# Two sequences' adapters joined, with one gate made in the call ahead, and the shared tiles' down products of the experts issued in sequence

## What is computed

```python
g = einsum('td,edf->tef', xt, Wg); u = einsum('td,edf->tef', xt, Wu)
h = silu(g) * u
y = einsum('tef,efd->ted', h, Wd)
out = einsum('ted,te->td', y, combine)
```

```python
gate = softmax(x.mean(axis=1) @ gate_w.T)
top_w, top_i = top_k(gate, 2); top_w = top_w / (top_w.sum(-1) + 1e-8)
h = gelu(x @ Wd[top_i] + bd[top_i], approximate=False) * top_w
out = h @ Wu[top_i] + (top_w * bu[top_i]).sum()
```

## Time and profile before

| | before |
|---|---|
| median of 3 runs | 3846.09 us (3843.22 to 3848.20) |
| the profiled execution | 3842.31 us |
| its span, first to last instruction | 3840.4 us |
| TensorE busy | 3608.5 us, 94% |
| VectorE busy | 2288.8 us, 60% |
| ScalarE busy | 1735.2 us, 45% |
| GpSimd busy | 824.6 us, 21% |
| mean granted clock of TensorE | 0.994 |

### The profile page before, as it was taken

The page is one execution under the profiler, slowest core; times in us unless marked ns, Lnnn a source line. Parts: engine busy times, 40 slices in busy tenths (PEclk is TensorE's granted clock), DMA queues, the critical chain, the costliest instruction groups (busy, mean ns, idle before and its releaser), DMA issues.

```text
span 3840.4 us, 78752 instructions
## 1 busy us (share of the span) xinstructions
PE 3608.5 (94%) x31071; PEld 2406.5 (63%) x31167; DVE 2288.8 (60%) x7514; ACT 1735.2 (45%) x3546; POOL 824.6 (21%) x1374
## 2 busy tenths in 40 slices
PE   6999999988999999998899999999889999999988
PEld 3656567666565667766556566776655656677665
DVE  4546455677654645577755554557675555455876
ACT  2425333466442523356644252335664335233656
POOL 3203023311210302332021030333302102033330
PEclk8999999999999999999999999999999999999999
DMA  3000000000000000000000000000000000000000
GB/s 88 1 1 2 1 1 1 2 1 2 13 1 1 2 1 1 1 2 2 1 13 1 1 2 1 1 1 2 2 7 8 1 1 1 1 1 1 2 2 9
DMA packets 27032, 17.47 MB, mean 5 GB/s; under 512 B 9425, under 2 KB 26274, under 8 KB 26658
## 3 DMA queue, kind: packets, MB, share of 16 engines
q1 hardware_dynamic: 26658, 12.32, 1.2%
HBM read 10.22 MB, written 2.10 MB: 3 GB/s over the span
## 4 chain that ended last, share of the span: by engine, by line
PE 71%; DVE 11%; POOL 7%; ACT 6%; issue 3%; SPq 1%; DVEq 0%; another core or an unknown queue 0%
PE banks L1237 9%; PE banks L1199 8%; PE banks L1204 8%; PE banks L1049 5%; PE banks L1088 5%; POOL work L564 5%; PE banks L1103 4%; PE banks L1028 3%; PE banks L1291 3%; PE banks L1499 3%; PE banks L1353 2%; ACT work L872 2%; ACT work L866 2%; PE banks L1512 2%; DVE work L1973 2%
## 5 line engine op out<-in xcount | busy, mean ns | idle before, releaser
L1684 DVE CUSTOM_DVE_ANT_0 work<-banks,mask_row 128x512 f32<-128x512 f32 (+3 forms) x1024 | 433.9, 486 | 279.3 <-PE banks L1049 279.2
L719 ACT ACTIVATE work<-banks 128x512 f32<-128x512 f32 x352 | 210.2, 597 | 672.2 <-PE banks L1199 657.0
L1775 DVE TENSOR_TENSOR work<-work,banks 128x512 f32<-128x512 f32 x352 | 242.1, 688 | 444.8 <-PE banks L1204 423.5
L520 POOL TENSOR_TENSOR rstd<-rstd,half 128x4 f32<-128x4 f32 x65 | 65.6, 1009 | 1948.2 <-DVE rstd L1608 1948.2
L742 ACT ACTIVATE work<-banks 128x384 f32<-128x384 f32 (+1 forms) x768 | 358.8, 534 | 252.2 <-PE banks L1088 251.6
L1237 PEld LDWEIGHTS banks<-wd,work 128*128 128x128 f32 (+2 forms) x4096 | 357.5, 189 | 179.9 <-issue 179.9
L1088 PE MATMUL banks<-work 32*128 32x512 f32 (+3 forms) x2048 | 443.7, 464 | 6.5 <-DVE work L1684 3.9
L1049 PE MATMUL banks<-work 32*128 32x384 f32 (+3 forms) x2048 | 405.2, 456 | 11.9 <-ACT work L728 6.4
L1237 PE MATMUL banks<-wd,work 128*128 128x128 f32 (+2 forms) x4096 | 376.6, 279 | 0.0
L531 POOL TENSOR_SCALAR_AFFINE_SELECT work<-work 128x128 f32<-128x128 f32 (+1 forms) x768 | 253.4, 333 | 458.8 <-ACT work L742 435.5
L1088 PEld LDWEIGHTS banks<-work 32*128 32x128 f32 x2048 | 243.0, 183 | 76.8 <-ACT work L742 39.4
(11 more groups left out here) (320 smaller groups left out, 6627.2 us busy)
## 6 DMA issues: line engine op xcount, KB each, us to landing
x_a<-in_L_attn_a_x_dram SPq DMA_DIRECT2D x5, 256.0 KB, 2.9
x_b<-in_L_attn_a_x_dram SPq DMA_DIRECT2D x4, 256.0 KB, 3.9
wg<-in_L_ffn_Wg_dram SPq DMA_DIRECT2D x2, 512.0 KB
wu<-in_L_ffn_Wu_dram SPq DMA_DIRECT2D x2, 512.0 KB
wd<-in_L_ffn_Wd_dram SPq DMA_DIRECT2D x16, 64.0 KB
out_dram<-x_a SPq DMA_DIRECT2D x4, 256.0 KB
out_dram<-x_b SPq DMA_DIRECT2D x4, 256.0 KB
wk_l<-in_L_attn_a_Wk_dram SPq DMA_DIRECT2D x1, 512.0 KB, 3.6
```

The source lines that it names most:

```text
L1684: m = eng.tensor_tensor_reduce(out=summed[:, k % 2, col:col + N], in0=bank(bk)[:, col:col + N], in1=mask_row[:, T - N:T], scale=1.0, scala ...
```

## The change

- **Adapters joined.** `pe_adapters`, `act_adapters` and `adapters` issue both calls of a pair as one piece. TensorE: down products of a, transpose of a's mix, six fills, the norm's transposes of b, bias and up products of three token tiles of a, gate product of b, the last up tile of a, down products of b, transpose of b's mix, bias and up products of b, and then the norm's transposes of the call behind. At the turn's end six fills stand before those.
- **a's gate in the call ahead.** `gate_pool`, `gate_logits`, `gate_rank` and `gate_weights` of call 0 are issued inside the second linear attention (`lin`, n = 1), those of call 2 at the end of the second relative attention (`rel`, n = 1), with the gate product (`gate_products`) on TensorE and Exp (`gate_exp`) on ScalarE in the same calls. The gate's buffers get places outside those calls' own. VectorE's rank and weights of call 2 stand ahead of the relative attention's addition to `x_b`.
- **Bias by TensorE.** The mixed bias starts the accumulation of each of the four token tiles (two instructions each); VectorE adds one bank of 512 columns to x, instead of the bias and two halves.
- **Shared tiles in sequence.** `DOWN_BEHIND` puts the down products of tiles 0, 1 and 2 behind the up product of tile 4, and those of 11, 12 and 13 behind that of tile 15. All others keep their lag of two tiles.

```diff
@@ -99,6 +99,10 @@
 NTILE = len(TILES)
 LAST = {e: max(i for i, parts in enumerate(TILES) if any(q[0] == e for q in parts)) for e in range(E)}
 DOWN_LAG = 2
+DOWN_BEHIND = [[] for _ in range(NTILE + 1)]
+for i in range(NTILE):
+    DOWN_BEHIND[min(4 + NTILE // 2 * (i // (NTILE // 2)) if len(TILES[i]) > 1 else i + DOWN_LAG, NTILE)].append(i)
 HSLOTS = 12

 LAYERS = ["attn_a", "moe_1", "attn_b", "moe_2", "lin_attn", "adapter_1", "rel_attn", "adapter_2"]
...
@@ -793,6 +792,8 @@
                     eng.activation(l_sq[:, i // 2 % 2, :], dst, ACT.Square).then_inc(l_sqr, 1)
                 if i == NC2 + 3:
                     act_norm(eng, lin_call(n) + 1, 7)
+            if n == 1:
+                gate_exp(eng, 0)
             eng.wait_ge(l_ssk, NC2 * n + NT)
             eng.activation(l_inv[:, 1, :, 0:H // 2], l_ssum[:, 1, :, 0:H // 2], ACT.Sqrt).then_inc(l_norm, 1)
             for i in range(NT):
...
-            eng.activation(d_wT[0:E, :], bank(6)[0:E, 0:P], ACT.Copy).then_inc(d_wTs, 1)
-            act_norm(eng, adapter_call(n) + 1, 0)
+            eng.activation(g["ex"], g["lg"], ACT.Exp, bias=g["negm"][:, 0:1],
+                           accum_out=g["z"][:, 0:1]).then_inc(d_exs, 1)
+        def act_adapters(eng, n):
+            def hidden_rows(m):
+                for k in range(KD):
+                    eng.wait_ge(d_dn, KD * m + k + 1)
+                    eng.activation(d_hids[:, m % 2, k, :], bank(k), ACT.Gelu, bias=down_b[:, k:k + 1]).then_inc(d_hs, 1)
+            def mix_column(m):
+                eng.wait_ge(d_wTp, m + 1)
+                eng.activation(gates[m // 2]["wT"][0:E, m % 2, :], bank(6)[0:E, 0:P], ACT.Copy).then_inc(d_wTs, 1)
+            hidden_rows(n)
+            mix_column(n)
+            act_norm(eng, adapter_call(n + 1), 7)
+            gate_exp(eng, n + 1)
+            hidden_rows(n + 1)
+            mix_column(n + 1)
+            act_norm(eng, adapter_call(n + 1) + 1, 0)

         def act_rel(eng, n):
             act_parts(eng, n, float(HD) ** -0.5)
...
@@ -885,6 +900,8 @@
                 if i >= 4 and i % 2 == 0:
                     group_columns(eng, n, NG * (4 + n) + i // 2 - 2, 7, a_pv, NG * n + i // 2 - 1)
             group_columns(eng, n, NG * (5 + n) - 1, 7, a_pv, NG * (n + 1))
+            if n == 1:
+                gate_exp(eng, 2)
             eng.wait_ge(a_oT, 4 + n + 1)
             eng.activation(xnTs[n % 2][:, :], bank(0), ACT.Copy).then_inc(a_oTs, 1)

...
@@ -1244,15 +1259,15 @@
                 if i >= 2 or n % 2 == 1:
                     moe_gate(eng, n, i)
                     moe_up(eng, n, i)
-                if i >= DOWN_LAG:
-                    down(i - DOWN_LAG)
+                for k in DOWN_BEHIND[i]:
+                    down(k)
                 if i == 9:
                     eng.wait_ge(m_acc, E * n + 1)
                     pe_norm(eng, moe_call(n) + 1, 7)
                 if i == 11 and n % 2 == 0:
                     moe_logits(eng, n + 1, 7)
-            for i in range(NTILE - DOWN_LAG, NTILE):
-                down(i)
+            for k in DOWN_BEHIND[NTILE]:
+                down(k)

         def pe_lin(eng, n):
             xnT = xnTs[n % 2]
...
@@ -1303,12 +1318,17 @@
                     eng.wait_ge(l_ssc, n + 1)
                 elif i == NT + 1:
                     eng.wait_ge(xnT_ok, lin_call(n) + 1)
+                    if n == 1:
+                        eng.wait_ge(d_lgs, 1)
                 elif i >= 2:
                     eng.wait_ge(l_vr, NC2 * n + i - 1)
                 eng.matmul(bank(value_bank(i)), xnT[:, P * (i % NT):P * (i % NT) + P],
                            wv_l[:, 512 * (i // NT):512 * (i // NT) + 512],
                            start=True, stop=True).then_inc(l_vp, 1)

+            if n == 1:
+                eng.wait_ge(xnT_ok, lin_call(n) + 1)
+                gate_products(eng, 0, 7)
             for i in range(NT):
                 key_rows(NT + i)
                 if i == 0:
...
+            def down(m):
+                eng.wait_ge(xnT_ok, adapter_call(m))
+                for k in range(KD):
+                    if m == 2 and k == 1:
+                        eng.wait_ge(d_lgs, m + 1)
+                    eng.matmul(bank(k), downT[:, k, :], xnTs[m % 2][:, :], start=True, stop=True).then_inc(d_dn, 1)
+            def mix_column(m):
+                eng.wait_ge(d_ws, m + 1)
+                eng.transpose(bank(6)[0:E, 0:P], gates[m // 2]["w"][:, m % 2, :], ident[:, :]).then_inc(d_wTp, 1)
+            def up(m, tiles):
+                out = [bank(4 + m % 2)[:, P * t:P * t + P] for t in range(NT)]
+                if tiles[0] == 0:
+                    eng.wait_ge(d_wTs, m + 1)
+                    for t in range(NT):
+                        eng.matmul(out[t], gates[m // 2]["wT"][0:E, m % 2, :], up_b[:, :], start=(t == 0), stop=False,
+                                   skip_group_check=True)
+                for t in tiles:
+                    for k in range(KD):
+                        i = eng.matmul(out[t], d_hids[:, m % 2, k, P * t:P * t + P],
+                                       gates[m // 2]["up"][:, m % 2, k, :], start=False, stop=(k == KD - 1),
+                                       skip_group_check=True)
+                if t == NT - 1:
+                    i.then_inc(d_y, 1)
+            down(n)
+            mix_column(n)
+            fill(eng, 5 if n == 0 else 7, 6)
+            pe_norm(eng, adapter_call(n + 1), 7)
             eng.wait_ge(d_hs, KD * (n + 1))
-            if adapter_call(n) + 1 < CALLS:
-                pe_norm(eng, adapter_call(n) + 1, 0)
             eng.wait_ge(d_ups, n + 1)
-            for t in range(NT):
-                o = bank(4 + t // 2)[:, P * (t % 2):P * (t % 2) + P]
-                for k in range(KD):
-                    m = eng.matmul(o, d_hid[:, k, P * t:P * t + P], d_up[:, k, :], start=(k == 0), stop=(k == KD - 1))
-                if t % 2 == 1:
-                    m.then_inc(d_y, 1)
-                if t == 0:
-                    eng.wait_ge(d_wTs, n + 1)
-                    eng.matmul(bank(7)[:, 0:P], d_wT[0:E, :], up_b[:, :], start=True, stop=True).then_inc(d_bias, 1)
-            if adapter_call(n) + 1 == CALLS:
+            up(n, (0, 1, 2))
+            eng.wait_ge(xnT_ok, adapter_call(n + 1))
+            gate_products(eng, n + 1, 7)
+            up(n, (3,))
+            down(n + 1)
+            mix_column(n + 1)
+            eng.wait_ge(d_hs, KD * (n + 2))
+            eng.wait_ge(d_ups, n + 2)
+            up(n + 1, (0, 1, 2, 3))
+            if adapter_call(n + 1) + 1 == CALLS:
                 fill(eng, 6, 6)
-                pe_norm(eng, CALLS, 0)
+            pe_norm(eng, adapter_call(n + 1) + 1, 0)

         def pe_rel(eng, n, w):
             pe_project(eng, n, w)
...
@@ -1541,6 +1580,8 @@
                 if i >= 2:
                     columns(2 * i - 3)
             weigh(NG - 1)
+            if n == 1:
+                gate_products(eng, 2, 1)
             group_rows(eng, n, NG * (5 + n) - 1, 7)
             pe_out(eng, 4 + n, rel_call(n), w[:, 3, :], bp_row, 0, lambda: fill(eng, 3, 2))

...
@@ -1822,6 +1861,10 @@
                     eng.tensor_copy(l_k[:, t, 512 * half:512 * half + 512], bank(2 + i % 2)).then_inc(l_kr, 1)
                     if i >= 1:
                         reduce_keys(i - 1)
+                    if n == 1 and i == 2:
+                        gate_pool(0)
+                    if n == 1 and i == 3:
+                        gate_logits(0, 7)
                     if i == NT + 1:
                         eng.wait_ge(l_ss, NC2 * n + NC2)
                         eng.tensor_copy(l_ssum[:, 0, :, :].rearrange("p t h -> p (t h)"),
...
                         scale_out(c - 1)
+                    if n == 1 and c == 4:
+                        gate_rank(0)
+                    if n == 1 and c == 5:
+                        gate_weights(0)
...
+            def gate_pool(n):
+                g = gates[n // 2]
                 eng.wait_ge(xnT_ok, adapter_call(n))
-                link(eng.tensor_reduce(pooled[:, 0:1], xnT[:, :], AX.X, ALU.add))
-                eng.tensor_scalar(pool_rep[:, :], pooled[:, 0:1].to_broadcast([P, P]), 1.0 / T, None,
+                link(eng.tensor_reduce(g["pooled"], xnTs[n % 2][:, :], AX.X, ALU.add))
+                eng.tensor_scalar(g["rep"], g["pooled"].to_broadcast([P, P]), 1.0 / T, None,
                                   ALU.mult).then_inc(d_pool, 1)
-                if adapter_call(n) + 1 < CALLS:
-                    norm_stats(adapter_call(n) + 1)
+            def gate_logits(n, bk):
+                g = gates[n // 2]
                 eng.wait_ge(d_gate_ok, n + 1)
...
+                link(eng.tensor_copy(g["lg"], bank(bk)[:, 0:E]))
+                eng.tensor_reduce(g["negm"], g["lg"], AX.X, ALU.max, negate=True).then_inc(d_lgs, 1)
+            def gate_rank(n):
+                g = gates[n // 2]
...
+            def gate_weights(n):
+                g = gates[n // 2]
```

(23 more changed lines are left out.)

120 lines of the change are left out of this document (38 added, 82 removed).

## The result

The changed kernel takes 3794.2 us (median of 4 runs, 3788.8 to 3799.2) against 3846.5 (4 runs): ratio 0.9865, 95% interval 0.9851 to 0.9878. Forecast were 3791 us, a range of 3776 to 3817, and "faster". Timed once more with the experiments it took 3796.9 against 3844.4, ratio 0.9874 (0.9859 to 0.9889). The profiled execution of the table's "after" took 3799.2 us.

The account below looks back on a forecast made before the run. The prediction took TensorE, busy 94% of the span, and the gaps between its instructions as the bound. Pairs 22.4, turn's ends 16.8 and experts 16 made 55 us, giving a median of 3791 us, range 3776 to 3817.

Parts of the forecast that it names:

- Pair in front of the relative attention: Joined adapters a and b there: 21.1 us in place of 26.9, a gain of 5.8 us per turn.
- The gate ahead costs 0.24 us per turn: Second linear attention: a's two gate products on TensorE charged at 0.24 us, VectorE's 3.74 us taken as covered by idle time.
- The rival of the short covers: Both attentions: VectorE's 3.74 us come out before the next masks or `x_b`, at most 30 us, 3821; chance 0.07.
- Relative attention: Second relative attention: the gate's 3.74 us after the heads cost nothing, with 0.2 us to spare.
- The turn's end: Last pair of a turn: after a 2 us wait, the eighteen fills begin 4.2 us earlier, 16.8 us over four turns.
- Experts: Shared tiles' down products in sequence: 0.50 us gained per group, 32 groups, 16 us, with ends at 12.5 and 25.
- neither nothing nor a full price: Experts' 64-to-24-row change: free, group gain 0.78 us, or a full way in and out, gain 0.39; 0.28 taken.
- The clock: Joined pairs: rival that the clock falls and the kernel is slower, chance 0.03; one fall a pair costs 16 us, 3807.
- a few us either way: Whole run: clock falls elsewhere move when everything shifts, six stretches of some 2 us each.
- The sum: Whole kernel: 22.4 + 16.8 + 16 = 55 us gained, 3791 us for the median; the forecast had chance 0.55.

Follow-up runs that it names:

- after: The changed kernel, with joined adapters, early gate, bias on TensorE and grouped shared tiles, against the kernel before: 3794.2 us against 3846.5, ratio 0.9865.
- the four edits: Changed kernel with a's rank and weights later, bias added by VectorE, a's turn-end addition before b's weights, b's mix transpose and copy earlier: 3774.0 us, ratio 0.9816.

## Why the prediction was right, point by point

- *Pair in front of the relative attention.* Right to 0.15 us (5.95 for 5.8), and each time on the way within 0.1. The run with a's own gate shows which part of the change carries it: 4.2 of the 5.95 us hang on the gate made ahead, and at the turn's end nearly all.
- *The gate ahead costs 0.24 us per turn.* This is the term that was mis-sized: 1.50. "In turns of the column loop in which it idles 3.28 us before `sum_states`" compared the 3.74 us of the gate with VectorE's idle time, both right, but took durations from a stretch in which GpSimd rested. Beside GpSimd's multiplications four operations were held 0.6 to 1.0 us each, and the masks behind them came late. Moving the operations removed 1.28 of it, which shows that their place was the cost; that the holds, and not the 3.74 us themselves, made it is read from the timeline, where both delays (0.24 and 1.04) are shorter than the holds in front of them (1.8 and 1.4). The rival of the short covers named the place; it came to 5 us in all, not 30.
- *Relative attention.* The 3.74 us at its end fit, as worked out: in turn 3 the rank starts at 2823.25, t = -3.24, the weights end at 2826.99, t = 0.50. The 0.46 us more in the relative attention of a were not foreseen. They are there in every kernel with the early gate and four bias products, and absent (0.1) once either goes. Their cause stays open.
- *The turn's end.* Right (4.1 to 4.4 for 4.2), with the wait of 1.43 where 2 were named. The addition moved forward shows that the chain of store, load and norm sets it; the run with the bias on VectorE points to a second chain, over `x_b`, close behind.
- *Experts.* 0.59 a group for 0.50: 19.0 us for 16. The change from 64 to 24 rows costs 0.20, not 0.28, and neither nothing nor a full price. The 0.28 was a choice between two ends that no row decided, so its nearness is luck. By the Trainium skill's rule (TensorEngine Tiling (Array Packing), Key Properties) every change of mode drains TensorE; the trace agrees that this one is paid too, at half the price.
- *The clock.* The rival had one fall in each joined pair, 2 us each. It came in part: in the profile of after one of the four pairs 1 holds a fall (turn 4, 22.61 for 20.98, 1.6 us), and one turn's end begins in one. The prediction read from the earlier trace rows that a wait can lower the clock; those rows show TensorE busy for 1.93 and 2.00 of 2 us. The waits stand in the windows of before ahead of them, with busy times of 0.51 to 1.14 of 2 (columns as in the earlier trace rows; 0.50 is the lower level, 1.2 GHz, 1.00 the upper, 2.4):
```profile
632.00:634.00 2.00, 0.78 (x2) 0.00 (x0) 1.50 (x3) 0.90 (x3) 0.90 (x1) 1.00 0.00 0
634.00:636.00 2.00, 0.94 (x6) 0.74 (x6) 2.00 (x5) 1.02 (x3) 1.64 (x2) 1.00 0.00 0
...
3482.00:3484.00 2.00, 0.51 (x3) 0.03 (x1) 1.50 (x4) 0.91 (x3) 0.60 (x1) 1.00 0.00 0
3484.00:3486.00 2.00, 1.14 (x10) 0.94 (x12) 2.00 (x4) 0.72 (x3) 1.94 (x2) 1.00 0.00 0
```
  Four windows of the changed kernel show a fall behind much shorter waits. It begins in the last products of the relative attention, at 950.8, and reaches into the down products of the turn's end; no wait of TensorE is longer than 0.7 us in the 4 us before:
```profile
948.00:950.00 2.00, 1.57 (x11) 1.14 (x12) 1.73 (x10) 0.86 (x2) 0.00 (x0) 1.00 0.00 0
950.00:952.00 2.00, 2.00 (x14) 1.88 (x13) 1.82 (x10) 1.02 (x1) 0.00 (x0) 0.69 0.00 0
952.00:954.00 2.00, 2.00 (x5) 0.97 (x5) 1.87 (x12) 0.00 (x0) 0.00 (x0) 0.50 0.00 0
954.00:956.00 2.00, 2.00 (x6) 1.00 (x5) 0.88 (x8) 1.41 (x3) 1.01 (x1) 0.96 0.00 0
```
  Over the whole run there are more falls: six behind the load phase before and seven with the experts' edit alone, nine to fourteen in all but one of the kernels with joined adapters (that with the 24-row tile in the middle has six). In the twelve profiles with joined adapters 19 of the 96 pairs, stretches to the next turn included, have a fall that begins in them; in the two with the adapters of before, none of 16. The counts suggest that joined pairs draw falls, in about one of five; no experiment isolates it. It would not explain the others: eight of after's ten lie outside the pairs, and why they are more than before stays open. In the profiles they cost 6.7 us more than those of before, which the forecast, with "a few us either way", left to the range.
- *The sum.* The whole came out close partly by luck. The experts gave 3.0 us more than forecast and the pairs in front of the relative attention 0.6 more, the early gate cost 5.0 more and the relative attention of a 1.8. That is 51.7 for 55; and that the first timing shows 52.3 is no confirmation to the microsecond, since the second shows 47.6.

## What to carry to other kernels

Joining two calls pays when the chain that held one of them is ready ahead: in pair 1 the joining gave 1.8 us, the early gate 4.2. When a moved operation is to hide in another engine's idle time, ask not only whether the time is long enough but who else reads there: small VectorE operations with two inputs beside GpSimd lasted as long as what GpSimd had begun. And when single edits are worth less than what the falls of the clock move, judge them by the stage they touch, then time them together: four edits of 4 to 8 us by their stages gave 23.

## What the runs showed of the hardware

- A two-input operation of 64 elements on VectorE took 1.26 us instead of 0.23 where a GpSimd operation of 512 columns had begun 0.09 us before it; `RECIPROCAL`, with one tensor to read, took 0.16 beside another.
- TensorE pays 0.39 us for the way from 128 rows to 64 or 24 and back, and 0.20 between 64 and 24 (an average over the four groups of a stage, the same in all eight stages).
- The same kernel had ten falls of the granted clock in one profile and eleven in another, in places that differ. Most falls make their stage 0.4 to 2 us longer; one in the experiment of the four edits made it 2.9 longer, and falls among waits cost next to nothing. Four runs of one kernel lie up to 11.5 us apart (3786.9 to 3798.3, without the fills).
- The first attention of the launch took 113.2 us in the profile of before and 115.0 in that of after, with the same instructions: the lower level of the load phase ended at 45.9 us in the one and at 49.6 in the other.
